# Mixture stage: earlier start, split pieces spread over steps, output products ahead of hidden products

## The reference

```python
# stage 1: x += tanh(g_xattn[0]) * resampler attention(ctx_1024, layernorm(x))
# stage 2: the mixture
xf = layernorm(x)                                    # [4096, 256]
probs = softmax(xf @ router_w + router_b)            # 64 experts
tw, ti = top_k(probs, 8); tw = tw / sum(tw)
routed = sum_e cw[:, e] * (silu(xf @ w1[e] + b1[e]) @ w2[e] + b2[e])     # e = 0..63, hidden 64
shared = sum_s silu(xf @ sw1[s] + sb1[s]) @ sw2[s] + sb2[s]              # s = 0, 1, hidden 512
x += tanh(g_ffn[0]) * (routed + shared)
# stage 3: x += tanh(g_xattn[1]) * causal attention of layernorm(x) onto ctx_1024
# stage 4: x += tanh(g_ffn[1]) * quantised conv feed-forward(layernorm(x))
```

## Time and profile before

| | |
|---|---|
| median of 3 runs | 3353.44 us (3353.08, 3353.44, 3362.2) |
| profiled execution | 3354.25 us, span of its records 3352.5 us |
| PE / PEld / DVE / ACT / POOL busy | 3113.9 / 2885.6 / 2460.4 / 1645.7 / 764.2 us |
| mean granted TensorE clock | 0.975 of full |

### The profile page before, as it was taken

The page is one execution under the profiler, slowest core; times in us unless marked ns, Lnnn a source line. Parts: engine busy times, 40 slices in busy tenths (PEclk is TensorE's granted clock), DMA queues, the critical chain, the costliest instruction groups (busy, mean ns, idle before and its releaser), DMA issues. The chain is left out here.

```text
span 3352.5 us, 63415 instructions
## 1 busy us (share of the span) xinstructions
PE 3113.9 (93%) x20868; PEld 2885.6 (86%) x20868; DVE 2460.4 (73%) x4826; ACT 1645.7 (49%) x3104; POOL 764.2 (23%) x1372
## 2 busy tenths in 40 slices
PE   4999999999999999999699999999999879999588
PEld 3999999999999999999577788998989778888476
DVE  5777777777777777777766777777778756666787
ACT  2555555555555555555333322222222256666587
POOL 2222222223222222221111111111111123332220
PEclk9999999999999999999799999999999889999799
DMA  3000000000000000000200222423333200000000
GB/s 93 16 14 11 12 15 11 11 14 12 13 14 13 12 9 14 14 6 3 57 5 5 72 89 82 118 92 112 93 87 93 68 1 1 0 0 0 26 20 32
DMA packets 117456, 113.94 MB, mean 34 GB/s; under 512 B 39823, under 2 KB 83144, under 8 KB 117192
## 3 DMA queue, kind: packets, MB, share of 16 engines
q1 hardware_dynamic: 117192, 110.62, 11.4%
HBM read 105.33 MB, written 5.24 MB: 33 GB/s over the span
## 5 line engine op out<-in xcount | busy, mean ns | idle before, releaser
L437 ACT ACTIVATE x_pth<-x_ps 128x512 fp32r<-128x512 f32 (+1 forms) x768 | 376.4, 528 | 252.4 <-PE x_ps L671 249.7
L956 ACT ACTIVATE moe_sil<-moe_ps,moe_b 128x512 f32<-128x512 f32 x256 | 176.4, 689 | 561.1 <-PE moe_ps L1110 552.1
L539 DVE TENSOR_TENSOR x_ptl<-x_ps,x_pth 128x512 fp32r<-128x512 f32 (+1 forms) x768 | 402.9, 552 | 32.6 <-ACT x_pth L437 20.5
L457 ACT ACTIVATE x_p<-x_p,x_nmx 128x1178 f32<-128x1178 f32 x256 | 327.6, 1280 | 131.6 <-DVE x_p L563 131.3
L1133 PE MATMUL moe_ps<-moe_w2z,moe_gh 128*128 128x256 f32 (+1 forms) x1280 | 370.0, 289 | 1.8 <-DVE moe_gl L1073 1.8
L563 DVE TENSOR_SCALAR_CACHE_REDUCE x_p<-x_ps 128x1182 f32<-128x1182 f32 x256 | 354.5, 1385 | 22.4 <-PE x_ps L682 13.0
L671 PE MATMUL x_ps<-ident,x_p 128*128 128x128 f32 x2560 | 365.7, 274 | 2.1 <-DVE x_ptl L539 1.8
L1133 PE MATMUL moe_ps<-moe_w2z,moe_gl 128*128 128x256 f32 x1280 | 362.0, 283 | 0.0
L1133 PE MATMUL moe_ps<-moe_w2l,moe_gh 128*128 128x256 f32 x1280 | 361.9, 283 | 0.0
L697 PE MATMUL x_ps<-x_pth,x_vh 128*128 128x256 f32 x1152 | 346.3, 301 | 0.0
L697 PE MATMUL x_ps<-x_ptl,x_vh 128*128 128x256 f32 x1152 | 325.3, 282 | 0.0
(11 more groups left out here) (375 smaller groups left out, 8149.2 us busy)
## 6 DMA issues: line engine op xcount, KB each, us to landing
moe_gate<-moe_cw_rows SPq DMA_DIRECT2D x512, 128.0 KB, 2.9
xres<-in_x_dram SPq DMA_DIRECT2D x4, 1024.0 KB, 9.3
x_rawv<-in_L_xattn_Wkv_dram SPq DMA_DIRECT2D x16, 256.0 KB, 2.9
x_rawk<-in_L_xattn_Wkv_dram SPq DMA_DIRECT2D x32, 128.0 KB, 2.1
x_rawq<-in_L_xattn_Wq_dram SPq DMA_DIRECT2D x32, 128.0 KB, 2.2
x_rawo<-in_L_xattn_Wo_dram SPq DMA_DIRECT2D x32, 128.0 KB, 2.0
moe_w1r<-in_L_ffn_w_dram SPq DMA_DIRECT2D x8, 512.0 KB, 5.8
moe_w2r<-in_L_ffn_w_dram SPq DMA_DIRECT2D x4, 1024.0 KB, 10.1
```

Of the source, the lines that this page charges most:

```text
L437: act.activation(turn_dst(pth, x, lo, hi), turn_src(x, g), ACT.Copy).then_inc(hi_done, 1)
L457: act.activation(p[:, w % 4, DUP:DUP + R_KV], p[:, w % 4, DUP:DUP + R_KV], ACT.Exp, bias=nmx[:, w % 2:w % 2 + 1], scale=-1.0, accum_out=su ...
L539: last = dve.tensor_tensor(turn_dst(ptl, x, lo, mid), turn_src(x, g)[:, 0:mid - lo, :], turn_dst(pth, x, lo, mid).bitcast(F32), ALU.subtract)
L956: act.activation(dst[:, q % 2, :], ps[:, HID + q % 2, :], ACT.Silu, bias=bias).then_inc(silu_done, 1)
```

## The change

- Moments in the first stage: in the last batch of `resample_stage` VectorE makes the moments of tiles 0 to 23, two per fourth step, and those of tiles 24 to 31 behind the additions that finish them. ScalarE takes the root of the first 24 (w = 64), VectorE finishes `rstd` (w = 66) and normalises chunk 0 into the shared tile `z` (w = 67).
- A shared object `S` holds a buffer that is the resampler's `p`, the mixture's raw weights and the last stage's raw weights in turn, all four gates `tgs` (one tanh for all in the first stage), `z` and the moments. SP loads the raw weights of group 0 at the end of the first stage. The loads of the gates and their tanh go from the later three stages.
- Chunks turned within the first group: only chunk 0 is turned ahead. Chunk c + 1 is normalised by VectorE in q = 1 of chunk c, turned by TensorE in q = 4, kept by ScalarE in q = 4. The routing moves one step earlier: logits in q = 0 (from 1), their turn in q = 1 (from 2), the exponential in q = 3 (from 4), VectorE's four parts in q = 2 to 5 (from 3 to 6).
- Pieces: each weight matrix of a group is split in four pieces of 128 x 512. Groups 1 to 4 get theirs in the last chunk of the group before (q = 2: one, q = 4: two, q = 6: two) and in the first steps of their own (q = 0: two, q = 1: one).
- Outputs first: the step on TensorE is now P(q - 2), then H(q). At the change of a group, the last two P of the old group follow in the first two steps of the new one.

The core of the diff:

```diff
@@ resample_stage, DVE @@
+                    if head_of(u) == R_HEADS - 1 and not after:
+                        dve.wait_ge(y_added, U + 1 + ADD0)
+                        moments([TPB * b + 2 * (u % (TPB // 2)) + i for i in range(2)])
+                if not after and w >= 2 * TPB and w % 4 == 0 and w < STEPS:
+                    moments([(w - 2 * TPB) // 2 + i for i in range(2)])
+                if w == STEPS - 1 and not after:
+                    dve.wait_ge(x_moments, 2 * LATE + 4)
+                    dve.tensor_scalar(S.var[:, 0:LATE], S.mv[:, 0:LATE, 1], EPS, None, ALU.add).then_inc(stats, 1)
+                if w == STEPS + 2:
+                    dve.wait_ge(rooted, 5)
+                    newton_rsqrt(own, dve, S.var[:, 0:LATE], S.root[:, 0:LATE], S.rstd[:, 0:LATE])
+                if w == STEPS + 3:
+                    for t in range(TPC):
+                        dve.tensor_scalar(z[:, t, :], xres[:, t, :], S.mv[:, t, 0:1], S.rstd[:, t:t + 1], ALU.subtract, ALU.mult)
@@ resample_stage, SP @@
+            sp.wait_ge(turned, 3 * (STEPS * BATCH - 2) + TURN0)
+            load_moe_w1(sp, A, S, 0)
+            sp.wait_ge(turned, 3 * STEPS * BATCH + TURN0)
+            load_moe_w2(sp, A, S, 0)
@@ moe_stage @@
+        PIECES = [(0, 0), (0, 1), (1, 0), (0, 2), (1, 1), (0, 3), (1, 2), (1, 3)]
+        FIRST = {0: PIECES[3:5], 1: PIECES[5:7], 2: PIECES[7:]}
+        LATER = {(False, 2): PIECES[0:1], (False, 4): PIECES[1:3], (False, 6): PIECES[3:5],
+                 (True, 0): PIECES[5:7], (True, 1): PIECES[7:]}
@@ moe_stage, SP @@
             def weights(g):
-                if g:
-                    sp.wait_ge(w_split, 2 * g)
+                sp.wait_ge(w_split, NPC * g)
@@ moe_stage, ACT @@
+            w_high(0, *PIECES[0])
+            for k in range(KT):
+                act.wait_ge(turned, k + 1)
+                act.activation(xh[:, 0, k, :], ps[:, ROUTE + k, :], ACT.Copy).then_inc(first_high, 1)
+            for p in PIECES[1:3]:
+                w_high(0, *p)
+                    if g == 0 and q == 4 and not last_chunk(c):
+                        for k in range(KT):
+                            act.wait_ge(turned, KT * (c + 1) + k + 1)
+                            keep(c + 1, k)
+                    for p in pieces(g, c, q, before):
+                        w_high(*p)
@@ moe_stage, DVE @@
                     if q == LAG + 1 and before:
                         add_y(n - 1, c - 1, 1 - j)
-                    if g == 0 and 3 <= q < 7:
-                        route(c, q - 3)
+                    elif q == LAG + 1 and g:
+                        add_y(n - 1, CHUNKS - 1, 1)
+                    for p in pieces(g, c, q, before):
+                        w_low(*p)
+                    if g == 0 and not before:
+                        prepare(q)
+                    if g == 0 and q == 1 and not last_chunk(c):
+                        normalise(c + 1)
+                    if g == 0 and 2 <= q < 6:
+                        route(c, q - 2)
@@ moe_stage, PE, step @@
                     n = g * CHUNKS + c
-                    hidden(g, n, j, q)
-                    if g == 0 and q == 1:
-                        logits(n, lnT[:, :, bass.ds(c * CH, CH)])
-                    if g == 0 and q == 2:
-                        turn_logits(n)
                     if q >= LAG:
                         project(g, n, c, j, q - LAG)
                     elif before:
                         project(g, n - 1, c - 1, 1 - j, GB - LAG + q)
+                    elif g:
+                        project(g - 1, n - 1, CHUNKS - 1, 1, GB - LAG + q)
+                    hidden(g, n, j, q)
+                    if g == 0 and q == 0:
+                        logits(n, lnT[:, :, bass.ds(c * CH, CH)])
+                    if g == 0 and q == 1:
+                        turn_logits(n)
+                    if g == 0 and q == 4 and not last_chunk(c):
+                        pe.wait_ge(normed, c + 1)
+                        pe.wait_ge(shifted, c + 1)
+                        turn(c + 1)
                     if g == 0 and q == GB - 1:
                         turn_weights(n)
@@ ctx_attention_stage, SP (and alike in ffn_stage) @@
-            with nc.allow_non_contiguous_dma(reason="one column"):
-                sp.dma_start(tg[:, :], A["g_xattn"][1:2].partition_broadcast(P)).then_inc(d_in, 16)
-        ND = 8
+        ND = 7
```

## The result

The changed kernel takes 3492.26 us (median; 3490.83 to 3496.25) against 3356.53 us (3353.08 to 3362.2) before on the same chip: ratio 1.0406, interval 1.0389 to 1.0422. It is 136 us slower. The prediction said 3508, in 3425 to 3560. The profiled execution took 3492.43 us with a span of 3490.7, 138.2 more than before.

What follows compares the result with a forecast made beforehand. TensorE was taken to bound the kernel. Start -25.2, group 0 +18, late units +24, GpSimd +84 and +2.4, clock +46, group changes +2.6, rest +2.5 give +154.3 on 3354.25: 3508 us, range 3425 to 3560.

Steps and rivals of the forecast that it cites:

- The slack halves, and the chain does not fit: Between H and its P, the swap cuts slack from 5.64 to 2.82 us; the chain to `gl` needs 2.88.
- Ordinary late units: In routed chunks, every second unit's P waits for `gl`: 0.75 us per chunk, x32 = 24 us.
- The meeting with GpSimd: Once per routed chunk, GpSimd's copies delay `gh` and `gl`, making P(7) 2.72 us late: 31 x 2.72 = 84 us.
- The clock: Behind P(7)'s wait of about 2.5 us TensorE's clock halves for 3.40 us: 1.5 per gap, x31 = 46 us.
- Rival 1: TensorE's clock stays high in the 2.5 us gaps, dropping 46 + 4.5 us: 3458 us; chance 0.19.
- The start: From first stage to first H: 34.8 us earlier, chunk 0 of group 0 slower by 9.6; sum -25.2 us.
- Group 0, chunks 1 to 7: Routing-weight waits go, the next chunk's turn and late units come: +2.6 us per chunk, x7 = +18.
- rival 4: The waits pile up, with the low clock lasting longer and in group 0 too: 3575 us; chance 0.09.
- The changes of group: Where a group changes, 23.6 us won against late gates, low clock and other waits: net +2.6 us.
- The gate: After a group change, the gate fetch comes about 5.8 us late for its unit: 3 x 5.8 = 17.4, clock 4.5.
- Rivals 2 and 3: Routed chunks: swap costs nothing, 3309 us, chance 0.09; or only the GpSimd delay vanishes, about 3350 us, chance 0.05.

Runs made afterwards that it cites:

- lag_three: The changed kernel with P three units behind its H instead of two, `gh` and `gl` four deep, P still first in each step: 3337.6 us.
- short_copies: The changed kernel with GpSimd's `xh` and `xl` copies of groups 1 to 4 cut to 2 columns from 512, leaving tokens stale: 3386.77 us.
- gates_apart: hidden_first_late with the first stage's gate fetches taken off its inputs' queue and issued behind the first v, k and q weights: 3309.64 us.
- hidden_first: The changed kernel with only the swap undone, H before P again in each TensorE step: 3335.94 us.
- late_weights: The changed kernel with raw weights of groups 2 to 4 issued in chunk 6, unit 4 of the group before, instead of chunk 0: 3474.04 us.
- hidden_first_late: The changed kernel with H before P again and raw weights of groups 2 to 4 issued in chunk 6 of the group before: 3312.44 us.

## Why the prediction came out as it did

Sign, mechanism and place were right; the size was 16 us too large, for the most part because the clock fell less often than I counted. In order of its steps:

1. **The slack halves, and the chain does not fit.** Right. lag_three shows that it is the slack. Ordinary late units: 26.26 - 22.79 = 3.47 a chunk, of which the meeting's step takes 2.69 (5.51 instead of 2.82, from first H to first H), leaves 0.78; 0.75 was forecast. In short_copies they cost 1.2: the long wait beside GpSimd gives the unit behind it slack (its step takes 3.04 us in the changed kernel, chunk 1 of group 2, and 3.48 in short_copies), and without it more units are late. The two terms are not independent, which is why that run came 12 us above its expectation.
2. **The meeting with GpSimd.** Right, 2.69 a chunk for 2.72 forecast. There are 30 such waits and not 31. The Trainium skill's rule (SBUF — State Buffer, section "Who interferes with whom") has VectorE blocked for the whole of GpSimd's instruction. The trace agrees to 0.15 us: `gh` starts 0.39 us into `xl` and ends at 2232.86, 0.28 after it, less than the 0.43 that it takes alone, and as before. short_copies shows that these copies are what costs.
3. **The clock.** Right in what one fall costs (27.78 - 26.26 = 1.52, for 1.5), wrong in how often. I counted a fall behind each of 31 waits, from a gap of 1.9 us that left the clock high and two longer ones that did not. The length does not decide that: in lag_three_late the wait at the first of these places, 1.92 us up to 502.74, has a fall behind it (the clock is 0.50 from 504.2). In chunks 1 to 6 of groups 2 to 4 it fell in 13 of 18: these chunks cost 82.7 us more than before, that is 18 x 3.47 + 13 x 1.5 = 82.0. Over groups 1 to 4 it was low at the start of 24 of 32 chunks; one of the 24 is behind another wait (the first H of group 1, for `xl`, 2.79 us), so it fell behind 23 of the 30 meetings. Seven falls fewer at 1.5 are 10.5 of the 16 us. Within the meetings too the length does not tell which: 2.42 us left the clock at 1.00 (2153.34) and brought it to 0.50 (2379.49), and 2.72 us in chunk 0 of group 2 left it at 1.00. Rival 1, that it stays high, falls with it, though in a quarter of the chunks it was true.
4. **The start.** First H 30.4 us earlier for 32.8 forecast (34.8 less 2 for the longer first stage), chunk 0 of group 0 +8.4 for +9.6: -22.0 for -23.2. Here one error made up for another: the first stage's last additions came at 1630.12, 5.2 us later than before where 2 were forecast, and from there to the first H it took 5.7 us for 6.6. There is luck in it too: five of the seven kernels with this first stage have their first H 2.2 to 3.0 us later in their traces (gates_apart, above), with a clock that had fallen on the way there; here it had not.
5. **Group 0, chunks 1 to 7.** +10.2. Chunks 1 to 6 took 13.5 us more, which is 15.7 for seven of the kind, for +18 forecast; the other -5.5 are the change of group at the end of chunk 7. The number is near, the working is not. Chunks 1, 2 and 6 took only 1.4 to 1.5 us more each, for 2.6. Chunks 3, 4 and 5 took 3.0 to 3.1 more, because P waited for `gl` there (1.90, 2.06 and 1.89 us) and the clock fell behind it, a term that the forecast put at nothing outside rival 4. The wait in chunk 3 and what came behind it:

```profile
1749.81:1751.71 1.90, 0.00 (x1) 0.00 (x0) 1.67 (x4) 0.69 (x1) 0.21 (x1) 1.00 0.00 0
1752.71:1756.11 3.40, 3.40 (x12) 2.83 (x12) 1.73 (x4) 0.00 (x0) 0.00 (x0) 0.50 0.00 0
```

The like waits in chunks 1 and 2, 1.90 and 2.05 us, left it at 1.00.
6. **The changes of group.** The seam of groups 2 to 3 went from 16.88 to 15.97 even with the swap; hidden_first has 11.5 for the same work, as forecast. The gate took it back as forecast and a little more: steps of 8.82, 9.57 and 10.84 us where 2.82 is due, 6.0 to 8.0 each for 5.8. Its price with the clock is the 22.5 us that late_weights takes off the three chunks 0, for 21.9: right. In hidden_first the gate waits take back more than the seam had cost: chunk 7 of group 2 and chunk 0 of group 3 take 22.8 + 31.3 = 54.1, before 29.4 + 21.6 = 51.0.
7. **The sum.** Forecast +154.3 as -23.2 (start), +18 (group 0), +160.5 (groups and changes), -1; measured +138.2 as -22.0, +15.7, +144.1, +0.4. The term that was mis-sized is the clock in the third of these, by 10.5; one meeting fewer is 2.7, and the last 3.2 are in no one term that I can name.

Of what was to show it: P waits for `gl` 109.6 us (near 100), chunks of groups 2 to 4 of 27.5 to 27.9 us with the low clock but 26.3 in the others. Rivals 2 and 3 fell with the first chunk of group 2.

One seam remains in the fastest kernels. At the end of group 0 the first H of group 1 waits 4.24 us. The profile names no releaser, but it starts right behind the last of GpSimd's copies, which stand behind the last routing. hidden_first_late:

```profile
1858.91 0.60 ACT L1078 ACTIVATE moe_cwT<-moe_ps 128x512 fp32r<-128x512 f32 x1 [2.00 <-PE moe_ps L1287]
1859.81 0.66 POOL L1006 CAST moe_cws<-moe_cwT 128x512 fp32r x1 [24.78 <-ACT moe_cwT L1078]
1860.67 2.34 POOL L1010 TENSOR_TENSOR moe_xl<-moe_lnT,moe_xh 128x1024 fp32r<-128x1024 f32 x1 [0.21 <-POOL moe_cws L1006]
1863.11 0.77 PE L1231 MATMUL moe_ps<-moe_xh,moe_w1h 128*128 128x512 f32 x1 [4.24 <-issue]
```

`xl` ends at 1863.01 and H starts 0.10 later. `xl` does not read `cws`; putting `xl` ahead of `cws` for the first chunk was not tried.

## What to carry to other kernels

In a pipeline of two products on one engine, count the time between the end of the first and the start of its second; a swap in the step or one unit of lag moves it by a whole unit, and the waits of the profile before do not show it, because behind a chain that takes 5.39 of 5.64 us nothing waits; its timeline does. Take the longest chain of a period for the count, not the ordinary one: 2.88 against 2.82 cost 0.8 us a chunk, 5.39 against 2.82 cost 2.7 and, three times in four, another 1.5 for the clock. Where large transfers and small ones that are needed at once share a queue, issue the large ones where no small one is due for as long as they take; here that and the slack turned 3492 into 3312.

## What was unexpected of the hardware

A wait of about 2.4 us on TensorE brings the granted clock down in some cases and not in others: in 13 of 18 like chunks, at idle times of 2.41 to 2.45 us. Shorter waits did it too: 1.89 and 1.90 us in group 0, where another of 1.90 us did not; and 2.72 us in chunk 0 of group 2 did not. The same two waits of 2.3 us at the end of one and the same first stage brought it down in some kernels and not in others, and that goes with a first H 2 to 3 us later. So a gain of 1 us in that stage can't be read from one profile before the clock rows of both are compared. What decides whether it falls is open here. The Trainium skill's page "TensorE: Matmul & The Clock Gate" (section "Why this matters for your kernels") warns only of longer gaps; the falls here speak against that, and the 5 of 18 against my own rule that such a gap always does it.
